# Three scalings of a Householder step move from VectorE to ScalarE in a tridiagonalisation on one NeuronCore

## The reference

```python
def _L0_gnn_ref(features, A, W1, b1, W2, b2):
    deg = jnp.sum(A, axis=0) + jnp.sum(A, axis=1) - jnp.diagonal(A)
    d_inv_sqrt = jnp.where(deg > 0, jax.lax.rsqrt(deg), 0.0)
    L = jnp.diag(deg) - A
    L_norm = d_inv_sqrt[:, None] * L * d_inv_sqrt[None, :]
    _, U = jnp.linalg.eigh(L_norm)
    agg = jnp.einsum('mn,bnd->bmd', U.T, features)
    h = jax.nn.relu(agg @ W1 + b1)
    out = h @ W2 + b2
    return jnp.einsum('nm,bmd->bnd', U, out)
...
x = _layernorm(x + _L0_gnn_ref(x, adj, ...), axis=-1)
x = _layernorm(x + _L1_gnn_ref(x, adj, ...), axis=-1)   # an LSTM over windows of nodes
x = _layernorm(x + _L2_gnn_ref(x, adj, ...), axis=-1)
x = _layernorm(x + _L3_gnn_ref(x, adj, adj, ...), axis=-1)
```

## Time and profile before

| what | value |
|---|---|
| median of 3 runs | 2133.13 us (2132.79 to 2136.34) |
| the profiled execution's own time | 2133.11 us |
| its span in the profile | 2131.1 us |
| PE, DVE, ACT, POOL busy | 84%, 67%, 40%, 31% of the span |
| `tridiagonalise`, from the trace | 19.0 to 215 us of the span |
| mean granted TensorE clock | 0.943 |

### The profile page before, as it was taken

How to read it: one execution, slowest core, us unless ns; L and a number is a source line. 1 busy time by engine, 2 the same in 40 slices (tenths; PEclk the granted TensorE clock), 3 DMA queues, 4 the chain that set the end, 5 groups by cost and what they waited for, 6 DMA issues and landing times.

```text
span 2131.1 us, 32060 instructions
## 1 busy us (share of the span) xinstructions
PE 1790.4 (84%) x9764; PEld 1539.9 (72%) x9764; DVE 1434.7 (67%) x5781; ACT 852.5 (40%) x1766; POOL 664.6 (31%) x1058
## 2 busy tenths in 40 slices
PE   3445334426999999999999999999999999989998
PEld 2334333314989788888889999988888888768886
DVE  7999999985777565554444444444444677887886
ACT  2333122201344466333333333323323465756664
POOL 0001344402233366433333333333332111651221
PEclk9999766657999999999999999999999999999999
DMA  6000000000111000000000000000010311320111
GB/s 193 2 1 2 1 1 1 1 1 20 60 40 50 20 15 19 11 5 9 10 11 10 10 0 10 20 1 0 0 39 10 149 60 60 102 70 21 40 41 60
...
## 3 DMA queue, kind: packets, MB, share of 16 engines
...
q10 hardware_dynamic: 592, 0.17, 0.1%
...
## 4 chain that ended last, share of the span: by engine, by line
PE 67%; DVE 5%; ACT 3%; POOL 1%; issue 1%; ACTq 0%; another core or an unknown queue 0%; DVEq 0%; POOLq 0%
PE ps L2163 43%; PE ps L2552 4%; PE ps L1687 2%; PE ps L1712 2%; PE ps L2768 2%; PE ps L2754 2%; PE ps L1673 1%; PE ps L1697 1%; PE ps L1664 1%; PE ps L2808 1%; PE ps L2802 1%; ACT l_raw L1584 1%; DVE j_lnstats L1570 1%; PE ps L2791 1%; DVE x L1561 1%
## 5 line engine op out<-in xcount | busy, mean ns | idle before, releaser
L2294 ACT ACTIVATE l_gates<-ps,biases 128x512 f32<-128x512 f32 (+1 forms) x504 | 289.4, 636 | 490.3 <-remote 475.8
L2163 PE MATMUL ps<-l_nodes_in,l_even 128*128 128x512 f32 x1392 | 321.3, 390 | 2.7 <-DVE x L1561 1.9
L2163 PEld LDWEIGHTS ps<-l_nodes_in,l_even 128*128 128x128 f32 x1392 | 260.7, 188 | 59.2 <-DVE x L1561 2.7
L2163 PE MATMUL ps<-l_nodes_in,kept 128*128 128x336 f32 (+1 forms) x1280 | 298.1, 350 | 2.0 <-ACT l_gates L2294 1.9
L2395 DVE TENSOR_TENSOR l_gates<-l_gates 128x512 f32<-128x512 f32 (+1 forms) x72 | 50.3, 699 | 341.9 <-ACT l_gates L2294 341.9
L2075 POOL CAST l_nodes_in<-big 128x512 fp32r (+3 forms) x142 | 100.5, 737 | 549.4 <-remote 519.7
L2163 PEld LDWEIGHTS ps<-l_nodes_in,kept 128*128 128x128 f32 x1280 | 229.2, 188 | 27.4 <-issue 4.3
L2163 PE MATMUL ps<-l_state,l_even 128*128 128x512 f32 x960 | 223.3, 392 | 0.0
L2163 PEld LDWEIGHTS ps<-l_state,l_even 128*128 128x128 f32 x960 | 180.3, 188 | 39.8
L2078 POOL TENSOR_TENSOR l_nodes_in<-big,l_nodes_in 128x512 fp32r<-128x512 f32 (+1 forms) x142 | 200.4, 1432 | 5.7
L994 PE MATMUL ps<-w,sw_xT 128*128 128x128 f32 x256 | 60.0, 428 | 120.7 <-ACT sw_xT L858 120.7
...
## 6 DMA issues: line engine op xcount, KB each, us to landing
...
```

Source lines behind the costliest of these rows:

```text
L2163: return pe.matmul(ps[:, 4 * j + gate, 0:n], weight[w_part][:, at:at + 128].bitcast(F32R), src[:, part, k, 0:n].bitcast(F32R), start=start ...
L2294: act.activation(gates[:, j, gate, 0:n], ps[:, 4 * j + gate, 0:n], ACT.Tanh if gate == G else ACT.Sigmoid, bias=bias[:, gate * KD + j:gate ...
```

## The change

Three scalings are taken off VectorE and done by ScalarE behind `u_col`: `own` times `no_tail` becomes a tile `own_n`, and `b_u` and `b_p` are written by ScalarE with `beta` as the scale. `mixed` is then one operation, `y * b - own_n`, so `b_y` goes, and `row` subtracts it instead of adding it. `m` is made by two operations, `prod = signed2 * inv` and `m = prod + signed`, instead of one. `signed2` moves behind `inv`. Several waits are dropped because another wait already implies them. ScalarE makes `no_tail` for the last step too.

```diff
@@ VectorE
             def minus_update(i):
                 e = i + 1
-                dve.wait_ge(p_ready, i + 1)
                 dve.wait_ge(b_u_ready, i + 1)
...
-            def b_p(i):
-                dve.wait_ge(p_col_ready, i + 1)
-                tt(col("b_p", i), p_col[i % 2], col("beta", i), ALU.mult).then_inc(chain[0], mark("b_p", i))
-
...
-            def signed2(i):
-                dve.wait_ge(norm2_ready, i + 1)
-                after(("half_sign", i))
+            def x(i):
+                after(("b_pu", i))
+                dve.wait_ge(b_p_ready, i + 1)
+                stt(col("x", i), col("b_u", i), col("b_pu", i), col("b_p", i), ALU.mult,
+                    ALU.subtract).then_inc(chain[0], mark("x", i))
+
+            def signed(i):
+                dve.wait_ge(norm_ready, i + 1)
+                dve.reciprocal(col("inv", i), col("norm", i)).then_inc(chain[0], mark("inv", i))
+                if i == 0:
+                    after(("half_sign", i))
                 tt(col("signed2", i), col("norm2", i), col("half_sign", i),
                    ALU.mult).then_inc(chain[0], mark("signed2", i))
...
                 tt(col("signed", i), col("norm", i), col("half_sign", i), ALU.mult).then_inc(chain[0], mark("signed", i))
+                after(("signed2", i))
+                tt(col("prod", i), col("signed2", i), col("inv", i), ALU.mult).then_inc(chain[0], mark("prod", i))
...
+            def m(i):
+                after(("prod", i))
+                tt(col("m", i), col("prod", i), col("signed", i), ALU.add).then_inc(m_ready, 1)
+
...
-                after(("signed2", i), ("inv", i), ("signed", i))
-                stt(col("m", i), col("signed2", i), col("inv", i), col("signed", i), ALU.mult,
-                    ALU.add).then_inc(m_ready, 1)
                 dve.wait_ge(m_ready, i + 1)
-                dve.wait_ge(r_col_ready, i + 1)
                 tt(head, col("m", i), head, ALU.add).then_inc(chain[0], mark("head", i))
+                dve.wait_ge(no_tail_ready, i + 1)
                 dve.reciprocal(col("inv_m", i), col("m", i)).then_inc(chain[0], mark("inv_m", i))
...
-                dve.wait_ge(tail2_ready, i + 1)
                 after(("inv_m", i))
                 stt(col("b", i), col("tail2", i), 0.0, col("inv_m", i), ALU.is_gt,
                     ALU.mult).then_inc(chain[0], mark("b", i))
...
-                tt(col("beta", i), col("b", i), col("inv_head", i), ALU.mult).then_inc(chain[0], mark("beta", i))
-                if e < STEPS:
-                    ts(b_y[:, e + 1:], y[i % 2][:, e + 1:], col("b", i), None, ALU.mult).then_inc(chain[0], mark("b_y", i))
-                after(("beta", i))
-                tt(col("b_beta", i), col("b", i), col("beta", i), ALU.mult).then_inc(chain[0], mark("b_beta", i))
-                dve.wait_ge(u_ready, i + 1)
-                tt(col("b_u", i), col("u_col", i), col("beta", i), ALU.mult).then_inc(b_u_ready, 1)
+                tt(col("beta", i), col("b", i), col("inv_head", i), ALU.mult).then_inc(beta_ready, 1)
 
             def mix(i):
                 e = i + 1
-                dve.wait_ge(own_ready, i + 1)
-                dve.wait_ge(no_tail_ready, i + 1)
-                after(("b_y", i))
-                stt(mixed[:, e + 1:], own[i % 2][:, e + 1:], col("no_tail", i), b_y[:, e + 1:], ALU.mult,
-                    ALU.subtract).then_inc(chain[0], mark("mixed", i))
-                after(("uy", i), ("b_beta", i))
+                dve.wait_ge(beta_ready, i + 1)
+                tt(col("b_beta", i), col("b", i), col("beta", i), ALU.mult).then_inc(chain[0], mark("b_beta", i))
+                if e < STEPS:
+                    dve.wait_ge(own_n_ready, i + 1)
+                    stt(mixed[:, e + 1:], y[i % 2][:, e + 1:], col("b", i), own_n[:, e + 1:], ALU.mult,
+                        ALU.subtract).then_inc(chain[0], mark("mixed", i))
+                after(("b_beta", i))
                 tt(col("factor", i), col("uy", i), col("b_beta", i), ALU.mult).then_inc(chain[0], mark("factor", i))
@@ ScalarE
                 act.wait_ge(m_ready, i + 1)
-                act.wait_ge(r_col_ready, i + 1)
                 act.activation(col("u_col", i), ident[:, e:e + 1], ACT.Identity, bias=col("r_col", i),
                                scale=col("m", i)).then_inc(u_ready, 1)
+                if e < STEPS:
+                    act.wait_ge(no_tail_ready, i + 1)
+                    act.wait_ge(own_ready, i + 1)
+                    act.activation(own_n[:, e + 1:], own[i % 2][:, e + 1:], ACT.Copy,
+                                   scale=col("no_tail", i)).then_inc(own_n_ready, 1)
+                act.wait_ge(u_ready, i + 1)
+                act.wait_ge(beta_ready, i + 1)
+                act.activation(col("b_u", i), col("u_col", i), ACT.Copy, scale=col("beta", i)).then_inc(b_u_ready, 1)
+                act.wait_ge(p_col_ready, i + 1)
+                act.activation(col("b_p", i), p_col[i % 2], ACT.Copy, scale=col("beta", i)).then_inc(b_p_ready, 1)
```

More of the change, by code:

```diff
@@ L136, in tridiagonalise @@
     rows = [sb(f"row{i}", [N, N]) for i in range(2)]
-    mixed, b_y, minus_S = (sb(name, [N, N]) for name in ("mixed", "b_y", "minus_S"))
+    mixed, own_n, minus_S = (sb(name, [N, N]) for name in ("mixed", "own_n", "minus_S"))
     turned = [sb(f"turned{i}", [N, N]) for i in range(2)]
     junk = [sb(f"junk{i}", [N, N]) for i in range(4)]
-    names = ("norm2", "r_col", "half_sign", "signed2", "norm", "inv", "signed", "m", "inv_m", "inv_head", "tail2",
+    names = ("norm2", "r_col", "half_sign", "signed2", "norm", "inv", "signed", "prod", "m", "inv_m", "inv_head", "tail2",
              "no_tail", "b", "beta", "b_beta", "uy", "factor", "u_col", "b_u", "b_p", "pu", "b_pu", "x")
@@ L215, in r_col @@
                     col("r_col", i)).then_inc(r_col_ready, 1)
-            def signed2(i):
-                dve.wait_ge(norm2_ready, i + 1)
-                after(("half_sign", i))
-                tt(col("signed2", i), col("norm2", i), col("half_sign", i),
-                   ALU.mult).then_inc(chain[0], mark("signed2", i))
             def x(i):
-                after(("b_pu", i), ("b_p", i))
+                after(("b_pu", i))
+                dve.wait_ge(b_p_ready, i + 1)
                 stt(col("x", i), col("b_u", i), col("b_pu", i), col("b_p", i), ALU.mult,
@@ L291, in _ @@
                     minus_update(i - 1)
-                    b_p(i - 1)
                 norm2(i)
@@ L311, in _ @@
             last = STEPS - 1
+            after(("factor", last))
             b_pu(last)
             minus_update(last)
-            b_p(last)
             x(last)
```

31 lines of the change are left out of this document (13 added, 18 removed).

## The result

The changed kernel takes 2111.13 us (median of 4 runs, 2108.88 to 2112.18), against 2132.96 us before (median of 4, 2130.91 to 2136.34). The ratio is 0.9895 with a 95% interval of 0.9878 to 0.9912: about 22 us faster, where 18.3 us (2114.8 us) was forecast, inside the range of 2108.5 to 2123.

A forecast was written before the change was run, and what follows sets the result against it. VectorE was taken to set the pace in `tridiagonalise`. Savings of 0.05 and 0.25 us made 0.30 a step, 18.3 us over 61 steps, so 2133.1 falls to 2114.8 us, range 2108.5 to 2123.

The forecast's parts named there:

- What bounds the kernel: In `tridiagonalise` VectorE sets the pace; a microsecond gained in a step is a microsecond at the end.
- Part A: From the start of `row` to `head` in each step: 1.73 to 1.68 us, 0.05 saved, all through `b_p`.
- Rival 1: At `m`: GpSimd doesn't hold it, so 0.14 is saved before `head`; 2109.3 us, chance 0.10.
- Part B: From `head` to the next `row` in each step: 1.34 to 1.09 us, 0.25 saved.
- rival 2: At `b`: the dropped wait is worth nothing, its distance belongs to the reciprocal; 2119.1 us, chance 0.12.
- The place of `mixed`: Start of `mixed` counted from the start of `head` (H): from H+0.97 to H+0.72, `b_u` no longer between and one wait.
- The floor set by `p`: At `pu`: it can't start before H+0.95 (H is the start of `head`), so further VectorE gain there is worth nothing.
- The sum: 0.05 + 0.25 = 0.30 us a step, over 61 steps 18.3 us, giving 2114.8 us.
- Rival 3: At `prod`: GpSimd holds it too, so the step saves only 0.14 us; 2124.6 us, chance 0.12.
- Rival 4: ScalarE becomes the pace through late activations, slower than before; 2139.2 us at 0.65 late, chance 0.05.
- The bound of 0.39: On ScalarE: `b_u` is at worst as long as `u_col`, 0.39 us; the new activations were taken as covered.

The follow-up runs named there:

- cols-only run: The kernel before with only `b_u` and `b_p` made by ScalarE: 2130.36 us, ratio 0.9990.
- single-`m` run: The changed kernel with `m` made by one operation again (signed2 * inv + signed): 2113.18 us, ratio to before 0.9899.
- PSUM: The changed kernel with the column `prod` written to PSUM instead of SBUF: 2106.22 us, ratio 0.9872.
- small-GpSimd: The changed kernel with GpSimd's subtraction cut from 64 columns of `qT` to 1: 2106.15 us, ratio 0.9868.
- waits-only run: The kernel before with only the implied waits dropped, nothing moved to ScalarE: 2125.20 us, ratio 0.9968.
- all waits back: The changed kernel with all dropped waits put back: 2121.68 us, ratio 0.9948.
- `own_n` only: The kernel before with only `own_n` made by ScalarE and `mixed` as one operation, `row` subtracting it: 2121.39 us, ratio 0.9947.

## Why the prediction was right, point by point

**What bounds the kernel.** Right. VectorE sets the pace, the gain lies wholly inside `tridiagonalise`, and nothing behind it was waiting for a fixed time: 21.85 us there, 20.7 us in the span, 21.8 us between the medians.

**Part A: 0.05 us forecast, 0.06 measured in the middle step** (1.73 to 1.67) and 0.07 at both ends of the stage. The mechanism was right in each of its parts. `b_p` alone gave 0.06 (cols-only run). The split of `m` gave nothing, since `m` ends with GpSimd in either form (single-`m` run), and `prod` goes ahead of it. The move of `signed2` wasn't tried alone; that it gave nothing follows from the same hold. What a held operation waits for is shown by the PSUM and the small-GpSimd runs. The Trainium skill (SBUF — State Buffer, section on the two separate sides) says it of two SBUF inputs, and the trace agrees: 0.23 us for the sum with both in SBUF, 0.15 with one in PSUM. Rival 1, an unheld `m`, didn't come by itself in the changed kernel; forced, it was worth 0.07 us with the split `m` and 0.14 with the single one.

**Part B: 0.25 us forecast, 0.26 in the middle step.** `b` at 0.08 behind `inv_head` was the wait's doing, and rival 2 fell by the run that put it back. `own_n`, with two waits of `mixed` gone beside it, gave 0.14 alone. The place of `mixed` came out at H+0.71 (0.72 forecast), but one reason given for it was wrong. Before, `mixed` didn't stand at H+0.97 because of `b_u`'s slot. It waited for the end of `b_y` and came 0.13 behind it, and with `b_u` away it stayed there (cols-only run). The whole of part B held because `b_y` went in the same change.

The floor set by `p` was right too: from the twentieth step on part B stays at 1.08 to 1.09 us in the changed kernel (every eighth step apart), and `pu` starts 0.03 to 0.05 behind the end of `p`, though `mixed` gets narrower, where before part B fell from 1.38 to 1.27. The wait put back at `b` bears it out, with 0.08 us in the early steps and 0.02 in the last. How much a faster VectorE in part B would still give wasn't tried by itself.

**The waits.** The sum took them into account at `b` and `mixed` only, and left out those at `signed2`, `pu`, `head` and `minus_S`. The waits-only run bears this out: 0.11 us in part B, next to nothing in part A. `b` was sized rightly at 0.07. At `mixed` one wait fewer gave 0.03 there, and two waits more cost 0.03 with all waits back. `x`'s second wait costs nothing that shows: `r_col` follows at its old distance.

**Rival 3, `prod` held too**, didn't happen in the ordinary step, even with all waits back: its start is 0.08 to 0.09 ahead of GpSimd, not 0.07. It did happen where a stall had made `prod` late, in one step of the changed kernel and four with all waits back. **Rival 4, ScalarE late**, didn't either: the three activations last 0.28, 0.30 and 0.26 us in the step shown. The bound of 0.39 was too wide, and the sum is the same with it, as they are covered. The estimate by the Trainium skill (ScalarE: Activation LUTs, on what ACT_TABLE_LOAD costs), 0.28 to 0.31, is nearer; only `b_p`, which reads PSUM, is below it at 0.26.

**What was mis-sized.** The sum, 18.3 against 21.85 us inside the stage. About 2.4 us of the difference are the stalls, eleven before and one after, which the prediction didn't have: I had read one step in the middle, which has none. The other 1.1 us are 0.02 us a step: the middle step gave 0.32 (0.06 and 0.26), and one step read to 0.01 us can't tell 0.30 from 0.32. That the middle step stands so well for all of them is partly luck. An early step gave 0.36 (part A 1.83 to 1.77, part B 1.42 to 1.12) and a late one 0.25 (1.62 to 1.55, 1.27 to 1.09), and the two even out.

**What stays open** is why a point of the grid of 128 costs up to 0.38 us in one kernel and nothing in another. The kernels with many stalls run through their VectorE instructions faster (10.8 to 11.3 a us, `own_n` only among them, against 9.4 to 10.1 in those with few), and they carry more extra waits; no run changed the one without the other. That the instructions arrive too late is an argument from the grid and the packets, not a finding.
